# Self-attention heads in pairs: two 32-bit pieces, one maximum over two PSUM banks, every second unit of products issued twice

## The reference

```python
q = (x @ wq).reshape(B, T, H, D)                  # T = 2048, H = 16 heads, D = 16
lat = x @ w_down                                  # 128 wide
k = (lat @ wk_up).reshape(B, T, H, D)
v = (lat @ wv_up).reshape(B, T, H, D)
q, k = _apply_rope(q), _apply_rope(k)
scores = jnp.einsum('bqhd,bkhd->bhqk', q, k) * scale
allowed = pages[None, :] <= pages[:, None]        # pages of 64 positions: block-causal
attn = jax.nn.softmax(jnp.where(allowed, scores, min), axis=-1)
out = jnp.einsum('bhqk,bkhd->bqhd', attn, v).reshape(B, T, E) @ wo
```

## Time and profile before

| what | value |
|---|---|
| median of 3 runs | 823.3 us |
| profiled execution | 824.24 us, of which the span 822.5 us |
| mean granted TensorE clock | 0.961 of full |
| preamble, to the first unit of maxima | 0 to 74.8 us |
| first units until the first scores | 74.8 to 88.8 us |
| 16 groups of attention | 88.8 to 530.3 us |
| the rest (out projection, cross-attention, feed-forward) | 530.3 to 822.5 us |
| busy: PE, DVE, ACT, POOL | 755.3, 620.3, 427.4, 149.9 us |

### The profile page before, as it was taken

The page is one execution under the profiler, slowest core; times in us unless marked ns, Lnnn a source line. Parts: engine busy times, 40 slices in busy tenths (PEclk is TensorE's granted clock), DMA queues, the critical chain, the costliest instruction groups (busy, mean ns, idle before and its releaser), DMA issues. The chain is left out here.

```text
span 822.5 us, 12183 instructions
## 1 busy us (share of the span) xinstructions
PE 755.3 (92%) x4329; PEld 393.8 (48%) x4329; DVE 620.3 (75%) x1107; ACT 427.4 (52%) x879; POOL 149.9 (18%) x170
## 2 busy tenths in 40 slices
PE   8874887999999999999999998899868999999997
PEld 5431232333223333222333231287547888888886
DVE  4899687888998899999898760067614778778786
ACT  1552463676667776657777867822123333333353
POOL 2564000000000000000000000013141455555520
PEclk9986797999999999999999998999999999999999
DMA  7796321120000000000440000030001222222103
GB/s 209 207 266 202 87 76 39 33 59 27 1 2 2 1 2 2 1 2 0 158 142 1 2 0 2 3 110 1 0 1 41 80 81 80 80 80 80 40 1 103
DMA packets 27152, 47.32 MB, mean 58 GB/s; under 512 B 6112, under 2 KB 23008, under 8 KB 26336
## 3 DMA queue, kind: packets, MB, share of 16 engines
q1 hardware_dynamic: 25184, 43.94, 17.8%
q10 hardware_dynamic: 1920, 2.75, 1.2%
HBM read 38.16 MB, written 8.39 MB: 57 GB/s over the span
## 5 line engine op out<-in xcount | busy, mean ns | idle before, releaser
L486 DVE TENSOR_REDUCE part_max<-psum 128x1 f32<-128x512 f32 (+3 forms) x560 | 341.4, 669 | 55.0 <-PE psum L672 50.0
L591 ACT ACTIVATE probs<-psum 128x512 f32<-128x512 f32 (+3 forms) x640 | 293.7, 539 | 155.5 <-PE psum L697 154.5
L672 PE MATMUL psum<-k_stack,q_stack 96*128 96x512 bf16 (+4 forms) x640 | 214.9, 364 | 18.6 <-DVE psum L472 11.2
L697 PE MATMUL psum<-q_stack,k_stack 98*128 98x512 bf16 (+4 forms) x640 | 202.3, 357 | 13.1 <-DMA q_stack<-shift 11.3
L709 PE MATMUL psum<-probs,v_all 128*17 128x512 f32 (+3 forms) x1280 | 149.7, 540 | 0.3
L672 PEld LDWEIGHTS psum<-k_stack,q_stack 96*128 96x128 bf16 (+1 forms) x640 | 60.1, 99 | 171.9 <-DVE part_max L486 121.5
L697 PEld LDWEIGHTS psum<-q_stack,k_stack 98*128 98x128 bf16 (+1 forms) x640 | 60.9, 99 | 94.3 <-ACT probs L591 39.2
L1471 PE MATMUL psum<-ctx_part,qc_part 128*128 128x512 f32 (+1 forms) x384 | 84.7, 371 | 5.0 <-POOL qc_part L1253 4.1
L877 POOL MEMSET eps<- 128x4 f32 x1 | 0.1, 102 | 459.6 <-POOLq L273 459.6
L1545 PE MATMUL psum<-v_parts,p_part 128*128 128x512 f32 (+3 forms) x416 | 76.9, 341 | 0.0
L1471 PEld LDWEIGHTS psum<-ctx_part,qc_part 128*128 128x128 f32 x384 | 67.3, 192 | 18.9 <-issue 4.9
(11 more groups left out here) (140 smaller groups left out, 681.6 us busy)
## 6 DMA issues: line engine op xcount, KB each, us to landing
mask<-in_mask SPq DMA_DIRECT2D x16, 800.5 KB, 4.4
pieces<-k_stack SPq DMA_DIRECT2D x24, 256.0 KB, 5.0
q_stack<-pieces SPq DMA_DIRECT2D x24, 256.0 KB, 4.2
k_stack<-pieces SPq DMA_DIRECT2D x24, 256.0 KB, 4.7
x_sb<-in_x SPq DMA_DIRECT2D x4, 512.0 KB, 8.9
out<-x_sb SPq DMA_DIRECT2D x8, 256.0 KB, 2.2
q_stack<-in_ctxT SPq DMA_DIRECT2D x1, 1601.0 KB, 11.1
probs<-in_cos ACTq DMA_DIRECT2D x4, 256.0 KB
```

Of the source, the lines that this page charges most:

```text
L486: nc.vector.tensor_reduce(part_max[:, h:h + m, r, c:c + 1], src, axis=AX_X, op=ALU.max).then_inc(m_read, 1)
L591: nc.scalar.activation(probs[:, s % 2, h, col:BLK], s_bank[h][:, col:BLK], ACT.Exp, scale=ATTN_SCALE).then_inc(exp_done, 1)
L672: last = nc.tensor.matmul(out, q_stack[b][0:rows, g * G + h, r * P:(r + 1) * P], k_stack[c][0:rows, g * G + h, 0:keys], start=True, stop=True)
L697: nc.tensor.matmul(s_bank[h][:, col:BLK], k_stack[s // TPB][0:rows, g * G + h, (s % TPB) * P:(s % TPB + 1) * P], q_stack[b][0:rows, g * G ...
```

## The change

- The rotated numbers are cut into two pieces of 32 bits (fp32r) instead of three of bf16. `last_piece` is gone on POOL and DVE, and with it four of ACT's eight copies per block. A head takes 3 x 16 + 2 + 4 = 54 rows, and two heads stand in one stack, one in rows 0 to 53 and one in rows 64 to 117. `piece[1]` is made by DVE straight from `rot`.
- SP only sends pieces. POOL issues the loads (12 DMAs of 256 KB for a block, as many as before), the extra rows (4 a block) and the shifts (2 a group). Between rotating blocks it issues the loads of the block before; `load_late` puts the 16 DMAs of block 2 behind the shift of group 1, and those of block 3 behind the shift of group 4.
- A unit of maxima covers two heads at a time, one of each half of the array, in two banks, and DVE reduces both with one instruction. There are 6, 14, 22 and 30 units in a group instead of 11, 27, 43 and 59. Two pairs of banks alternate. Units of one pair with an odd number are issued twice (`products * 2`).
- The two parts of the maximum are made ahead of the turn (two small DVE operations), so that one copy stays behind it (one instead of two).
- Scores come in pairs of heads over three banks instead of four. The entries are due after each of the two pairs and none after `weigh`. AHEAD and TURN_LAG are about half as large.
- 32 warming matmuls of 512 columns stand between the preamble and the attention; the waits for the stack of block b+1 move from the start of block b to its third group.

```diff
-Q_PIECES = [0, 0, 0, 1, 1, 2]
-K_PIECES = [0, 1, 2, 0, 1, 0]
+Q_PIECES = [0, 0, 1]
+K_PIECES = [0, 1, 0]
+PIECES = 2
+PAR = 2
+HP = H // PAR
+ROOM = P // PAR
...
-TURN_LAG = 3
-AHEAD = [(10, 10), (14, 14), (18, 18), (24, 24)]
+TURN_LAG = 2
+AHEAD = [(5, 5), (7, 7), (9, 9), (12, 12)]
...
-    s_bank = [banks(psum, h) for h in range(G)]
-    o_bank = banks(psum, 4)
-    m_bank = [banks(psum, n) for n in (5, 6, 7)]
+    S_BANKS = 3
+    s_bank = [banks(psum, n) for n in range(S_BANKS)]
+    o_bank = banks(psum, 3)
+    m_pair = [banks(psum, n, PAR) for n in (4, 6)]
...
+            def load(tb, n, which=(0, 1)):
+                pool.wait_ge(piece_sent[n][tb % 2], 32 * (tb // 2 + 1))
+                for s in which:
+                    load_piece(nc.gpsimd, io, (q_stack, k_stack)[s][tb], s, tb, n, stack_loaded[tb])
+            def send_shift(b, g):
+                pool.wait_ge(shift_done, index(b, g) + 1)
...
+                    nc.gpsimd.dma_start(dst, src).then_inc(shift_sent, 16)
...
             for tb in range(NB):
                 rotate(tb)
-                last_piece(tb)
                 if tb == 0:
                     norm(3)
+                if tb:
+                    for n in range(PIECES):
+                        if tb < NB - 1:
+                            load(tb - 1, n)
...
+            for k, (b, g) in enumerate(order):
+                if k:
+                    send_shift(b, g)
+                if k in (1, NG):
+                    pool.wait_ge(shift_sent, 16 * PAR * (k + 1))
+                    load_late(2 + k // NG)
...
-            def last_piece(tb):
-                for u in (2, 3):
-                    dve.wait_ge(piece_done[1], tb * 4 + u + 1)
...
+                        src = pair.rearrange("p (v x) -> p v x", v=PAR)[:, :, 0:m * keys]
+                        dst = part_max[:, :, r, c:c + 1].rearrange("p (v a) o -> p v a o", v=PAR)
+                        nc.vector.tensor_reduce(dst[:, :, heads[0]:heads[0] + m, :],
...
+                    if at >= 2:
+                        pe.wait_ge(m_read, at - 1)
                     if what == "unit":
+                        heads, r, c, keys = units[b][n]
+                        products = [(m, at_h, par) for m, at_h in enumerate(heads) for par in range(PAR)]
+                        for m, at_h, par in products * (2 if n % 2 and len(heads) == 1 else 1):
+                            h = g * (G // PAR) + at_h
+                            out = pair[:, par * BLK + m * keys:par * BLK + (m + 1) * keys]
+                            rows = slice(par * ROOM, par * ROOM + (STACK if c == b else TERM_ROWS))
+                            last = nc.tensor.matmul(out, q_stack[b][rows, h, r * P:(r + 1) * P],
+                                                    k_stack[c][rows, h, 0:keys], start=True, stop=True)
...
-            def scores(b, g, s, h):
+            def scores(b, g, s, half):
                 n = s_base(b, g) + s
                 col = first_col(b, s)
-                if n:
-                    pe.wait_ge(exp_done, (n - 1) * G + h + 1)
+                heads = range(half * PAR, half * PAR + PAR)
+                taken = n * G + heads[-1] + 1 - S_BANKS
+                if taken > 0:
+                    pe.wait_ge(exp_done, taken)
...
-                    for h in range(G):
-                        scores(*where, s, h)
-                        due = len(entries) * (sum(weights[:i]) + weights[i] * (h + 1) / (G + 1)) // sum(weights)
+                    for half in range(G // PAR):
+                        scores(*where, s, half)
+                        due = len(entries) * (sum(weights[:i]) + weights[i] * (half + 1) / (G // PAR)) // sum(weights)
                         maxima(entries[done:int(due)])
                         done = max(done, int(due))
                     weigh(b, g, s - 1 if s else steps[b] - 1)
...
+            pe.wait_ge(xt_copied, NB * EC)
+            for n in range(32):
+                nc.tensor.matmul(x_bank[n % 2], warm[:, 0:P], warm[:, P:P + BLK], start=True, stop=True)
```

More of the change, by code:

```diff
@@ L237, in self_attention @@
     starts = [sum(len(p) for p in parts[:n]) for n in range(len(parts))]
-    part_banks = [[1 if n == len(p) - 1 and n % 3 == 0 else n % 3 for n in range(len(p))] for p in parts]
-    bank_of = sum(part_banks, [])
-    def since(n, at):
-        at += starts[n]
-        return next((d for d in range(1, at + 1) if bank_of[at - d] == bank_of[at]), None)
     def entries_of(b, g):
         k = b * NG + g
-        for at, (what, kk, n) in enumerate(parts[k + 1]):
-            yield what, *order[kk], n, starts[k + 1] + at, since(k + 1, at), m_bank[part_banks[k + 1][at]]
+        for at, (what, kk, n) in enumerate(parts[k + 1], starts[k + 1]):
+            yield what, *order[kk], n, at, m_pair[at % 2]
     def s_base(b, g):
@@ L469, in _ @@
                     norm(tb + 2)
-            last_piece(NB - 1)
             nc.vector.memset(o_bank, 0.0).then_inc(o_cleared, 1)
             def maxima(entries):
-                for what, b, g, n, at, _, bank in entries:
+                for what, b, g, n, at, pair in entries:
+                    bank = pair[:, 0:BLK]
                     dve.wait_ge(m_ready, at + 1)
@@ L663, in maxima @@
             def maxima(entries):
-                for what, b, g, n, at, since_last, bank in entries:
-                    if since_last is not None:
-                        pe.wait_ge(m_read, at + (1 - since_last))
+                for what, b, g, n, at, pair in entries:
+                    bank = pair[:, 0:BLK]
+                    if at >= 2:
+                        pe.wait_ge(m_read, at - 1)
                     if what == "unit":
-                        for h, r, c, keys, col in units[b][n]:
-                            out = bank[:, col:col + keys]
-                            rows = STACK if c == b else TERM_ROWS
-                            last = nc.tensor.matmul(out, q_stack[b][0:rows, g * G + h, r * P:(r + 1) * P],
-                                                    k_stack[c][0:rows, g * G + h, 0:keys], start=True, stop=True)
+                        heads, r, c, keys = units[b][n]
[6 more added lines that the diff above has]
+                                                    k_stack[c][rows, h, 0:keys], start=True, stop=True)
                         last.then_inc(m_ready, 1)
                     elif what == "turn":
-                        pe.wait_ge(neg_max_done, index(b, g) + 1)
-                        nc.tensor.transpose(bank[0:G * TPB, 0:P], neg_max[:, :], ident[:, :]).then_inc(m_ready, 1)
+                        pe.wait_ge(neg_parts_done, index(b, g) * 2 + 2)
+                        parts_in = neg_parts[:, :, :, :].bitcast(F32).rearrange("p v n q -> p (v n q)")
+                        nc.tensor.transpose(bank[0:shift.shape[0], 0:P], parts_in, ident[:, :]).then_inc(m_ready, 1)
                     else:
@@ L794, in fold @@
     x2_t, row_fill, w_tern = keep["x2_t"], keep["row_fill"], keep["w_tern"]
[L795 removed]
+    front = front_views(keep["q_room"])
     wo, cw_q, cw_k, cw_v = (front[name] for name in ("wo", "cw_q", "cw_k", "cw_v"))
@@ L1597, in build @@
                 keep["v_parts"] = same_place.enter_context(nc.sbuf_tensor("v_parts", [P, S2_TILES, 2, E], F32R))
-            first_stacks = [sbo(f"q_stack{b}", [P, H, BLK], BF16) for b in range(NB - 1)]
+            with ExitStack() as same_place:
+                keep["q_room"] = [same_place.enter_context(nc.sbuf_tensor(f"q_room{b}", [P, HP, BLK], F32))
+                                  for b in range(NB - 1)]
+            first_stacks = [sbo(f"q_stack{b}", [P, HP, BLK], F32R) for b in range(NB - 1)]
             with ExitStack() as early:
```

242 lines of the change are left out of this document (107 added, 135 removed).

## The result

The changed kernel takes 938.2 us (median of 4 executions, 936.87 to 943.71), the kernel before 823.9 beside it: a ratio of 1.140 [1.135, 1.145]. I had forecast 846, and a range up to 890: the direction was right, the size wrong by 92 us.

The account below looks back on a forecast made before the run. DVE was taken to bound blocks 0 to 2, PE block 3, ACT the last group. 441 + 18 + 11 - 441.5 = +29, with -4 and -2 +23: 846 us; 8 in 10 range 798 to 890.

Parts of the forecast that it names:

- The new wait: In each step the second score pair waits 1.23 us for its own step's first exponential; a full step takes 2.97 us.
- DVE's maxima: One DVE reduction over 1024 elements takes 1.14 us, for 1.22 before; a block 3 group's units take 34.7 us.
- or DVE's time where that is longer: Rule for each group: its chain of 8.8, 20.7, 32.6 or 44.4 us by block, or DVE's time if longer.
- Second issues: Issuing every second unit twice costs 0.23 us in a step's second slot, 0 to 26 in all; 13 counted.
- Stalls: PE's waits for shifts: 3.9 and 4.2 us ahead of groups 4 and 15, 7 behind group 1; 18 in all.
- that rival: POOL issues slowly, at 1.2 us a DMA: preamble +14, stall behind group 1 +10, 870 us; chance 16%.
- POOL's queue: Skill rule: first byte after about 1 us against sync's 0.6, so four exposed shifts land 0.4 later each, under 2 us.
- Preamble and first units: Before the attention: preamble -4 us, first maxima -2, first scores near 83 us.
- The clock: PE spends 30 us at the low clock in chain-bound groups, costing 11 us.
- A low clock that lasts for whole groups: Sign that the forecast is wrong: PE's low clock lasts for whole groups.
- a rival at 13% and 905: Clock stays low after a stall; blocks 1 and 2 at 4.8 us a step add about 60: 905 us, chance 13%.
- groups: The 16 attention groups sum to 435 us, 441 with closing copies, for 441.5 before from first scores to last copy.

Follow-up runs that it names:

- e_four_fill: e_four_spread with unread matmuls ahead of the shift waits of groups 1, 2, 3, 4 and 15, and 44 warming ones before the first scores: 860.3 us.
- e_four_spread: Changed kernel with four score banks, one-bank units issued once, the order of the kernel before, and POOL's late loads spread over groups 1 to 10: 859.3 us.
- e_fill: Changed kernel with 60 instead of 32 warming matmuls, and unread matmuls ahead of the shift waits of groups 1, 2, 3, 4 and 15: 950.8 us.
- e_spread: Changed kernel with POOL's late loads spread over groups 1 to 10 instead of in bursts behind groups 1 and 4: 935.7 us, ratio 1.129.
- four-bank kernels: Changed kernel with four score banks, one-bank units issued once and the order of the kernel before: 869.9 us; with POOL's late loads spread, 859.3 us.
- e_gap_pairs: e_fill with units in a step's first slot issued four times, others once, and three unread matmuls in that gap in group 15: 907.6 us.
- held: Table column for e_gap_pairs, the changed kernel with unread matmuls ahead of shifts and first-slot units issued four times: 907.6 us.
- e_between_single: e_between with every unit of maxima issued once: 925.0 us, ratio 1.121.
- e_between: Changed kernel with the weighing moved between the two pairs of scores instead of behind both: 912.9 us, ratio 1.106.

## Why the prediction was wrong

**What a microsecond of low clock costs.** Low time is 2 x (1 - mean clock) x span. The executions of one kernel differ in it, and their times with it: e_four_fill from 154 to 171 us low and 857.3 to 863.2 us, e_four_spread from 177 to 205 and 853.2 to 862.9, e_fill from 209 to 242 and 943.9 to 953.9. One common slope fitted inside 13 kernels (47 executions of the changed kernel and the experiments) is 0.31, within 0.05 either way. The steps give nearly the same: 2.65 at 2.4 GHz and 4.10 at 1.2 GHz lose 1.45 in 4.10, 0.35. So does one group at two clocks: group 8 takes 36.4 us at 0.88 in the changed kernel and 33.5 at 1.00 in e_spread, 0.34; group 13 of the four-bank kernels gives 0.32. The changed kernel's profiled execution has 236 us low (0.874 of 934.7), before's 64 (0.961 of 822.5): 172 x 0.31 = **53 us**. The 53 are worked out, not isolated; e_gap_pairs, which takes that low time away, is 31 faster and carries the added matmuls.

**By the prediction's steps:**
- *The new wait*: right. 1.24 us for 1.23; at full clock 2.88 and 3.15 us a step for 2.86 and 2.97; pairs 0.23 apart (four pairs in 1.09, so (1.09 - 0.39) / 3). Groups 5, 8, 9, 12, 13 and 15, held at full clock, lie within 1.7 us of the forecast.
- *DVE's maxima*: the size was right (one takes 1.23 us and two in a row 2.36, so 1.13 apart for the forecast 1.14), but the rule "or DVE's time where that is longer" failed. A group's time was not the larger of chain and DVE: with two pair-buffers a unit waits for DVE in a slot on which scores and weighing hang. Windows of groups 10 and 11 in the changed kernel:

```profile
348.38:387.36 38.98, 33.45 (x237) 13.14 (x239) 31.78 (x37) 23.99 (x50) 1.10 (x2) 1.00 0.01 1
387.36:428.63 41.27, 34.21 (x243) 13.33 (x243) 35.73 (x37) 23.98 (x49) 1.10 (x2) 0.98 0.01 1
```

  DVE works for 31.8 and 35.7 us, as counted (33.1, 34.7), and stands for 7.2 and 5.5. By the table that is 5.5 and 6.2 there; in groups 6 (27.2 held, 21.1 forecast) and 7, 6.1 and 4.6: **22 us** in four groups, at full clock. In these four the weight loads of units wait for DVE for 3.4 to 7.3 us in the changed and the held kernel, in groups 5, 8, 9, 12 and 13 for 2.0 at most. They are also the groups with more than two units in a step (27 and 31 reductions in the 12 steps of groups 10 and 11, 23 in those of 8 and 9), which the forecast's step, made for two, did not count; no run separates the two causes.
- *Second issues*: wrong in sign, +13 counted; without them the kernel was 6 to 9 us slower, and 12 with the weighing between the pairs, through the clock. There are also 32 such units for four groups and 128 in all, not 28 and 112: by the forecast's own working half of 29 us, 15.
- *Stalls*: right in sum, 17.8 us for 18. The 7 behind group 1 were 8.67, by landing and not by issue; POOL's issue is 0.5 us, so that rival falls. Ahead of groups 4 and 15 they were 3.10 and 3.08 for 3.9 and 4.2. On POOL's queue a shift lands in 1.9 us (median) for 1.7 on SP's, 0.2 later and not 0.4, with 8 KB for 4.
- *Preamble and first units*: right. The first unit came at 69.93 for 74.77 (-4.8, forecast -4), the first scores at 82.46 for about 83. (POOL's 4 x 1.41 + 12 x 0.62 is 13.1 and not 13.3, which changes nothing.) Behind the 32 warming matmuls PE stood 6.12 us for DVE, so the clock was at 0.50 when the units began (70 to 72 us).
- *The clock*: **the step that failed.** "I count 30 us at the low clock in chain-bound groups: 11 us" became 172 us more than before, and 53. I took the clock to fall at stalls and to come back as in the earlier trace rows, under a PE that is then busy. The wait that I forecast myself leaves PE idle in every step, 0.22 us ahead of the second pair in the step shown and 0.75 in the last group. In that pattern the clock came back late (178 us) and fell without a stall. Behind group 15's stall it was back at 503 us before, 6 us on; in the changed kernel it did not come back within the group's 59.8 us. A low clock that lasts for whole groups was one of the signs of being wrong that I had named, and it came. I had this as a rival at 13% and 905, for blocks 1 and 2 only; it was block 0 and group 15, and parts of most others. Its 60 us were too few by my own numbers: the 221 us forecast for blocks 1 and 2, at 4.8 a step for 2.97, are 136 more, less where DVE bounds. The Trainium skill, "TensorE: Matmul & The Clock Gate", section "A second HAM failure mode: psum-queue depth-cycling", tells of a PE that idles briefly between groups of matmuls as it cycles through banks, often enough to make the clock oscillate; the trace agrees, and I should have weighed it.

**Where the 112 us of span went** (934.7 - 822.5). Clock 53. The forecast's other terms (groups, stalls, preamble) 12. DVE in groups 6, 7, 10, 11: 22. That leaves about 25, which are not settled: the waits for DVE in block 0, on diagonals and in group 14 (51.5 held, 46.8 with its stall forecast) are the candidates, and the slope's own 0.05 moves the clock's term from 45 to 62.

The four-bank kernel turns this round: it takes away both the wait inside the pair and the units of two banks, 68 us. It also changes their order, so the 68 are those of the whole edit. That its own residue is clock is shown by groups (equal at full clock, longer only where it is low) and agrees with the slope (a median of 200 us low, 136 more than before, 42 us, for 35); the attempts to remove it by added matmuls did not show it: held at 0.942 the kernel still took 855.7, so by that run part of the residue may be the kernel's own.

## What to carry to other kernels

Count which bank each matmul's wait frees before giving an engine lighter work: here three banks for pairs put one exponential into every step, and lighter DVE and PE work could not use it. A forecast whose own chain leaves PE idle in every step must price the whole stage at both clock levels, not only the stretches after stalls. And a time "the larger of chain and engine" was 22 us too low in four groups, where two pairs of banks let DVE run ahead little and steps held more than two units: count the units of each step, and add part of both times.

## What the hardware showed unexpectedly

- The clock fell from 1.00 to 0.50 within a group that had no wait above 0.97 us (e_fill, about 601.6 us), and stayed there for the 46 us to its end.
- Removing redundant matmuls made a kernel slower, 925.0 us for 912.9 (e_between_single, e_between).
- A shift of 8 KB took about 8 us to land behind 256 KB loads already issued by the same queue, and 1.9 in the median of all 32.
- Whole-array matmuls between half-array ones lengthened a step from 2.88 to 3.21 us at full clock, though they took no more array time (3 x 0.23 for 0.69 of three extra pairs).
